# Cross-attention of a decoder layer: scores five heads and masked maxima four heads ahead of the weighing, instead of four and three

## The reference, cut to what matters

```python
q = x @ Wq + bq
kv = context @ Wkv + bkv
k, v = jnp.split(kv, 2, axis=-1)
q = _larope(q, Lq); k = _larope(k, Lk)          # after the split into 16 heads
scores = jnp.einsum('bhqd,bhkd->bhqk', q, k) * 64 ** -0.5
scores = jnp.where(context_mask[:, None, None, :], scores, -jnp.inf)
attn = jax.nn.softmax(scores, axis=-1)
out = jnp.einsum('bhqk,bhkd->bhqd', attn, v)
return out.transpose(0, 2, 1, 3).reshape(B, Lq, H * hd) @ Wo + bo
```

## Time and profile before

| | us |
|---|---|
| median of 3 runs | 2001.78 (2001.27 to 2001.8) |
| profiled execution | 1998.29 |
| its span, first to last instruction | 1996.5 |
| cross-attention's pipeline, first scores to last values product | 526.8 to about 847 in the span |
| mean granted TensorE clock | 0.969 of full speed |

### The profile page before, as it was taken

How to read it: one execution, slowest core, us unless ns; L and a number is a source line. 1 busy time by engine, 2 the same in 40 slices (tenths; PEclk the granted TensorE clock), 3 DMA queues, 4 the chain that set the end, 5 groups by cost and what they waited for, 6 DMA issues and landing times. The chain is left out here.

```text
span 1996.5 us, 33819 instructions
## 1 busy us (share of the span) xinstructions
PE 1756.9 (88%) x11070; PEld 1100.6 (55%) x11070; DVE 1445.9 (72%) x2729; ACT 1055.5 (53%) x2220; POOL 995.8 (50%) x740
## 2 busy tenths in 40 slices
PE   7957887889889999898799999897889989998799
PEld 4333444444566676644444444444744746665699
DVE  6769999995578788749667666664764368886893
ACT  4776667672587787733666566564322231114342
POOL 1269889892462222004577777775000028664342
PEclk9979999999899999989899999999999989999899
DMA  2033443432587666241166575734830053335540
GB/s 72 0 125 111 138 139 127 123 129 78 119 174 157 160 143 162 68 128 38 45 210 205 191 220 171 238 100 121 276 99 1 17 166 119 137 116 180 197 142 17
DMA packets 138164, 257.47 MB, mean 129 GB/s; under 512 B 30661, under 2 KB 94822, under 8 KB 135318
## 3 DMA queue, kind: packets, MB, share of 16 engines
q1 hardware_dynamic: 120358, 212.16, 35.8%
q0 software_dynamic: 13824, 37.77, 6.3%
q10 hardware_dynamic: 3808, 5.38, 1.2%
HBM read 205.82 MB, written 49.44 MB: 128 GB/s over the span
## 5 line engine op out<-in xcount | busy, mean ns | idle before, releaser
L2355 POOL TENSOR_TENSOR soft_power<-soft_logit,soft_high 128x1024 f32<-128x1024 f32 x28 | 66.2, 2366 | 289.4 <-DVE soft_high L2429 289.0
L3211 PE MATMUL moe_up_ps<-moe_w_tile,ahead 128*64 128x352 f32 x1152 | 189.3, 471 | 1.3 <-issue 1.0
L3148 POOL DMA_INDIRECT moe_y<-ahead,moe_where x144 | 159.7, 1109 | 59.3 <-issue 40.2
L3355 ACT ACTIVATE moe_w_tile<-moe_w 128x1216 f32 x144 | 175.1, 1217 | 24.3 <-issue 18.9
L1791 ACT ACTIVATE xattn_prob<-xattn_sm,xattn_least 112x375 f32<-112x375 f32 x256 | 154.9, 606 | 52.4 <-DVE xattn_least L1692 47.6
L1692 DVE CUSTOM_DVE_ANT_0 xattn_sm<-xattn_s_ps,wide 112x375 f32<-112x375 f32 x256 | 137.8, 543 | 52.5 <-PE xattn_s_ps L1574 27.7
L3142 POOL DMA_INDIRECT ahead<-moe_tok,moe_where x144 | 147.2, 1022 | 56.9 <-issue 43.3
L1584 PE MATMUL xattn_pt_ps<-ident,xattn_prob 112*125 112x112 f32 x768 | 130.7, 279 | 24.1 <-ACT xattn_pt L1797 13.5
L1023 POOL TENSOR_TENSOR mamba_x_state<-mamba_x_state,mamba_cx_all 128x896 f32<-128x896 f32 x64 | 133.9, 2092 | 26.7 <-DVE mamba_x_state L1081 26.7
L1584 PEld LDWEIGHTS xattn_pt_ps<-ident,xattn_prob 112*125 112x125 f32 x768 | 111.9, 188 | 63.9 <-ACT xattn_prob L1791 42.9
L1017 POOL TENSOR_TENSOR xn<-mamba_u,mamba_b_all 128x896 f32<-128x896 f32 x64 | 133.7, 2092 | 14.6 <-DMA mamba_b_all<-mamba_b 14.6
(11 more groups left out here) (454 smaller groups left out, 4275.2 us busy)
## 6 DMA issues: line engine op xcount, KB each, us to landing
moe_w<-moe_w SPq DMA_DIRECT2D x64, 480.0 KB
soft_w<-soft_w SPq DMA_DIRECT2D x16, 1024.0 KB, 7.3
mamba_b_all<-mamba_b SPq DMA_DIRECT2D x32, 448.0 KB, 3.7
mamba_cx_all<-mamba_c SPq DMA_DIRECT2D x32, 448.0 KB, 3.7
mamba_cy_all<-mamba_c SPq DMA_DIRECT2D x32, 448.0 KB, 4.4
moe_w_tile<-moe_y SPq DMA_DIRECT2D x14, 1024.0 KB, 7.9
soft_logits<-soft_logit SPq DMA_DIRECT2D x28, 512.0 KB, 2.8
soft_logit<-soft_logits SPq DMA_DIRECT2D x14, 1024.0 KB, 5.1
```

The costliest lines, as they stand in the source:

```text
L3148: pool.indirect_dma_start(y_dram, bass.IndirectOffsetOnAxis(ap=where[:, 1, t:t + 1], axis=0), y_sb[:, 2 * s + i], None).then_inc(y_stored[ ...
L3211: mm = pe.matmul(up_ps[n * HALF:(n + 1) * HALF, i, 0:2 * I], xT[:, s % 2, at:at + HALF], w_tile[:, s, i, n, h * 2 * I:(h + 1) * 2 * I], st ...
L3355: place_weights = weight_placer(act, 0, lambda to, src: act.activation(to, src, ACT.Copy))
```

## The change

PE makes the scores of head h + 5 in slot h instead of h + 4, and DVE the masked maximum of head h + 4 instead of h + 3. ACT's exponents stay at h + 3, the turns at h + 2, the copies at h + 1. Ahead of the first batch PE makes five scores instead of four and DVE four maxima instead of three. Buffers, waits and all other steps stay.

```diff
                 def batch(b, s):            # PE
                     for h in range(NHEAD):
-                        ahead(b, s, h + 4, scores)
+                        ahead(b, s, h + 5, scores)
                         ahead(b, s, h + 2, turn_probs)
...
                 pe.wait_ge(q_kept, 3)
-                for h in range(4):
+                for h in range(5):
                     scores(0, 0, h)
...
                 def batch(b, s):            # DVE
                     for h in range(NHEAD):
-                        ahead(b, s, h + 3, bias_scores)
+                        ahead(b, s, h + 4, bias_scores)
                         if (h + 1) % QUAD != QUAD - 1:
                             ahead(b, s, h + 1, copy_probs)
...
-                for h in range(3):
+                for h in range(4):
                     bias_scores(0, 0, h)
                 copy_probs(0, 0, 0)
```

## The result

The changed kernel takes 1993.63 us in the median of 7 runs (1990.13 to 1996.67), the kernel before 2001.78 beside it (7 runs, 1997.13 to 2002.63). The ratio is 0.9962, interval 0.9948 to 0.9976: faster by about 0.4%, 8 us. The forecast was 1992.6. The profiled execution took 1990.13 us, 8.2 less than that of before. The time agrees better than the reasons do: two terms of the sum were half of what was measured, and one part that was to gain gained nothing.

A forecast was written before the change was run, and what follows sets the result against it. Steady batches were taken as bound by the context's DMA loop, with PE stalls on ACT. Gains of 3.2, 2.0, 0.3, 1.0, 1.7 and 1.0 made 9.2 us: 2001.78 - 9.2 = 1992.6, range 1989 to 1996, wider 1985 to 1999.5.

The forecast's parts named there:

- T moves 0.32 forward: T, the end of a batch's last values product, comes 0.32 us earlier as stalls in slots 10 and 11 go.
- the loop: Batches 3 to 12: values product, context load, keys, next values product set the time; gain 10 x 0.32 = 3.2 us.
- ACT's sequencer issues the load 0.25 later: Context load issued 0.25 us after T, landing 4.1 later, so slot 0's keys start at T + 4.35.
- slot 15 at T + 1.6: Turn of slot 15, after ACT's values copy, exponents and head 15 copy: T + 1.6 instead of T + 2.30.
- PE's way is T + 3.3: PE's own path to the next batch's keys, without the DMA: T + 3.3, before it T + 4.01.
- the keys' wait 1.1 us: Slot 0's wait for the context grows from about 0.4 to about 1.1 us per batch, PE's largest idle.
- batches 1 and 2 ... 2 x 1.0: Batches 1 and 2, set by ACT: ACT is 1.0 us earlier in each, 2.0 together.
- the tail, 3.7: Batches 13 to 15, no context transfer in front: gains of 1.0, 1.7 and 1.0 us.
- That ACT itself is the bound: Rival 1: PE waits for ACT, not the maxima; slots 10 and 11 stay; 1999 us; chance 0.15.
- the context lands earlier or later: Rivals 2 and 3: landing at 3.3 gives 1984 us, chance 0.13; at 4.8 gives 2000, chance 0.12.
- the third rival's own rule: Context landing later: each 0.1 us costs 1.1 us over 11 batches; chance 0.12, half of it slower.
- the third of my conditions: Sign that the forecast is wrong: DVE's maxima begin to wait for exponents.

The follow-up runs named there:

- The halves alone: Kernel before with only PE's scores five ahead, ratio 0.9971, or only DVE's maxima four ahead, ratio 1.0211.
- Both repeats of the changed kernel: The changed kernel run a second and a third time, unaltered, against the kernel before in the same group: ratios 0.9926 and 0.9921.
- the moved cast: ACT's cast of queries put behind the copy of head 15 in slot 14: on the changed kernel ratio 0.992, on the kernel before 0.9987.
- issue-ahead kernel: Kernel before with ACT's wait for T and the context load moved in front of the exponents of slot 13: ratio 1.0002.
- the first group: Runs of the kernel before again (1999.34 us), the changed one again (0.9926) and the two with a third context buffer alone (0.9971, 0.991).

## Why the prediction was right, and where it was not

**Right: what ACT's wait was and what it kept back.** Slots 10 and 11 lost their stalls (0.32), scores and maxima moved free of cost together, ACT's wait on maxima fell below 8 us (to 2.5), slot 15 kept 0.6, the cast of keys is now bound by POOL, 0.51 each. The halves alone show that the whole of it takes both moves.

**Wrong: "T moves 0.32 forward ... This is the gain that the loop keeps", 10 x 0.32.** A batch of the loop gained 0.66 in the seam shown: 0.48 from the keys to T (15.46, 635.45 to 650.91, against 14.98, 634.48 to 649.46) and 0.18 from T to the keys (4.27 against 4.09). Of the 0.48, slots 10 and 11 are 0.32, as listed. Twice 0.07 more stood between a turn and the weighing behind it, which my list of places left out: in slot 7 and in slot 11 (0.48 before, 0.41 after; in slot 11 648.09 to 648.57 and 646.72 to 647.13). Over all steady seams it is the same: 15.45 from the keys to T before, 14.99 after, and from T to the keys 4.40 and 4.52 in the two profiles of the kernel before, 4.15, 4.24 and 4.04 in the three of the changed one. The term of 0.32 a batch measured 0.68 (19.81 to 19.13).

**Wrong: "ACT's sequencer issues the load 0.25 later".** I carried the 0.25 over as a constant. It was a wait of the kind that the change removes. In the kernel before, the issue (631.43) stands in ACT's stream behind the exponents of the next head 0, which start at 631.38 when DVE's maximum for them has ended:

```profile
630.71 0.55 DVE L1692 CUSTOM_DVE_ANT_0 xattn_sm<-xattn_s_ps,wide 112x375 f32<-112x375 f32 x1 [0.91 <-PE xattn_s_ps L1574]
```

After the change these exponents have started 0.47 before T, and the issue follows T by 0.03. The issue comes 0.22 earlier after T in each batch of the loop, beside the stalls. The kernel with the issue ahead of the exponents shows the 0.04 by itself.

**Wrong in size: slot 15 at T + 1.6, so that PE's way is T + 3.3 and the keys' wait 1.1 us.** The turn came at 632.36, T + 1.97. ACT's values copy did not start at T + 0.1 but at T + 0.45. Until T + 0.23 (630.41 + 0.21) ACT was still at the exponents of the next head 0, and then it stood idle for 0.22 behind the issue of the DMA itself, which takes 0.37. That is nearly all of the 0.37 between 1.6 and 1.97. So PE's own way came forward by 0.33 only (T + 4.01 to T + 3.68), where the forecast had 0.7, and the context's landing, for which it had nothing, came forward by about as much, 0.22 of it through the earlier issue.

The keys' wait did not grow to 1.1. In the row it went from 3.9 us in 9 batches to 4.8 in 10, and by spacing from 0.26 to 0.41 at the seam shown (634.48 less 632.36 less 1.71). Over the ten steady seams the spacing gives 0.39 and 0.50 in the two profiles of the kernel before, and 0.47, 0.56 and 0.36 in the three of the changed one: no growth that stands out of the spread. My mark for failure was that the wait does not grow, and by it this step failed.

**Wrong: "batches 1 and 2 ... 2 x 1.0".** ACT was ahead there too, but in each of the four profiles with the new order and the cast in its old place the clock fell to the 1.2 GHz level at two of the three seams of the opening: always at the end of batch 2 (between 591 and 601 us), and at the end of batch 0 or of batch 1 (between 550 and 577). It did so in none of the five with the old order, nor in the three with the new order and the copy ahead of the cast. (Windows of the halves alone stand at 0.91 to 0.95 there.) What a fall costs can be read from mark to mark. From slot 2 of batch 1 to slot 2 of batch 2 the kernel before takes 20.90. Both repeats of the changed kernel keep their clock there and take 19.91, so the forecast's 1.0 is there. The lengths with a fall, of this batch and the next, are 21.4 to 22.3: 1.5 to 2.4 more than 19.91. With two falls in each profile that gives back 3.1 to 3.9 us, more than the whole opening was to gain.

That the fall needs the wait for the copy, with the cast in front of it, is shown by the moved cast: clock 1.00 and an opening 4 to 6 us shorter. Part of that is the shorter wait itself, which gave 1 to 2 us with the old order. Why the old order kept its clock is open: its waits at the end of batch 2 were 0.89 and 1.45 us, those of the new order 0.49 and 1.45, so the length of the waits doesn't tell the two apart. Nor does it tell the seams of one profile apart: the changed kernel, run again, has 0.48 and 1.44 at the end of batch 1 and keeps its clock, and 0.49 and 1.44 at the end of batch 2, where it falls. A kernel that varies that length alone was not tried.

**Low: the tail, 3.7 against 4.6.** I held back 1.1 of batch 15's stalls of 2.1, for DVE as the next bound. The marks part the three batches: they gained 1.14, 1.55 and 1.99 (19.14 to 18.00, 18.64 to 17.09, 17.16 to 15.17), where the forecast had 1.0, 1.7 and 1.0. So the low term is batch 15's, and what I held back for DVE was held back without need: all 2.1 of its stalls went, or nearly. The two repeats have the same lengths within 0.1.

**The rivals.** That ACT itself is the bound would have left slots 10 and 11 standing; they don't. That the context lands earlier or later fell as well: 4.1 in the median as before, and 4.0 to 4.3 from issue to keys in the mean of the steady batches, in every profile of the two kernels. The Trainium skill's page "DMA: Bandwidth & Descriptors" (section "Anatomy of one DMA — SWDGE (gpsimd) path") gives a fit for transfers that GpSimd issues, by which this one would take 2.9 us, an estimate. This trace doesn't bear it out for a queue of ACT's beside other traffic: 3.2 at least, 4.1 in the median.

**Luck.** The time came out right because the errors cancel: 3.2 too little for the steady batches and 0.9 for the tail, 3.3 too much for the opening. The stage was 0.9 off for that reason alone. The total had more help, from an experts' stage that happened to be 3.0 longer. The two later ratios, 0.9926 and 0.9921, would put the median at about 1987 and 1986, outside the 1989 to 1996 of the forecast itself, though inside the wider range.

**Slips in the working.** By the 0.16 measured for other slots, slot 14 stood 0.48, not 0.58 (a turn at 631.17, the scores at 631.49, the next turn at 632.13), and by the third rival's own rule 5.5 us of landing gives 2008, not 2007. Nothing else hangs on either.

**New: DVE's maxima wait for exponents.** The row reads 7.8 us in 20 times, 4.5 in 8 in the same row of before, so by the third of my conditions the step would be in doubt. It cost nothing that shows: PE's turns wait for DVE's copies in no row of these waits.

## What to carry to other kernels

When two engines hand work to each other through few banks, move both by the same step: here the scores alone gave -0.3%, the maxima alone +2.1%, and the two together -0.4 to -0.8%. A short delay in the profile between a release and the issue of a DMA (0.25 us) is not a cost until one has looked at what the issuing engine was waiting for just before, and an issue in its turn holds up the engine's next instruction (0.37 us long here, 0.22 of it idle time of ACT). In a loop that closes through a transfer, work out both ways around: with the two 0.3 us apart, the earlier issue alone brought nothing, since it made the other way as long, and this change, which shortened both, 0.2 us a batch beyond its own stalls.

## What was not expected of the hardware

- An ACT instruction behind a DMA issue waits for it: the copy of the values started 0.05 us after the issue of 0.37 us had ended (630.42 + 0.37 to 630.84), with its input ready at 630.39 and ACT idle from 630.62. It is so in eight of the ten steady batches, and in the issue-ahead kernel the exponents start 0.12 after the issue's end in all ten.
- The granted clock fell to its 1.2 GHz level with no single wait of PE over 1.50 us just before, and the order with waits of 0.89 and 1.45 us at the same seam stayed at 2.4 GHz.
- The releaser that a row names can be the wrong one: in the issue-ahead kernel the exponents at 652.36 are put down to PE's turn, though they start 0.12 after the DMA issue of 651.85 has ended (651.85 + 0.39).
- The experts' stage, with the same instructions, took 391 to 401 us from profile to profile within the first group: as much as the whole effect of the change. In the other two groups it took 458 to 470.
